# Order of the rough pieces, place of the shift row and PSUM operands on VectorE in a two-layer attention kernel

## The reference

```python
# x: (4, 128, 64, 64); per image N = 4096 positions, C = 128 channels
# layer 0: 64 inner channels
g     = einsum('ic,bcn->bni', g_w, xf) + g_b
theta = einsum('ic,bcn->bni', theta_w, xf) + theta_b
phi   = einsum('ic,bcn->bin', phi_w, xf) + phi_b[:, None]
p     = softmax(einsum('bni,bim->bnm', theta, phi), axis=-1)
y     = einsum('bnm,bmi->bni', p, g).transpose(0, 2, 1)
mid   = einsum('ci,bin->bcn', W_w, y) + W_b[:, None] + xf
# layer 1: 128 channels, x is mid
q, k, v = Wq x + bq,  Wk x + bk,  Wv x + bv
out   = x + softmax(q^T k * 128 ** -0.5) v
```

## Time and profile before

| what | value |
|---|---|
| median of 3 executions | 3499.48 us (3497.35 to 3500.27) |
| the profiled execution | 3494.88 us |
| its span, first to last instruction | 3493.1 us |
| mean granted TensorE clock | 0.991 |
| busy: PE, PEld, DVE, ACT, POOL | 3376.9, 2104.6, 2234.2, 1678.5, 2985.2 us |
| share of the chain that ended last | PE 89%, issue 4%, DVE 3%, POOL 2%, ACT 1% |

### The profile page before, as it was taken

One profiled execution on the slowest core, in us unless ns is written; L12 is line 12 of the kernel. 1 busy time (PEld: TensorE's weight loads), 2 busy tenths in 40 slices (PEclk: granted clock), 3 DMA queues, 4 the chain that ended last, 5 costly groups with the idle time before them and its releaser, 6 DMA issues.

```text
span 3493.1 us, 46688 instructions
## 1 busy us (share of the span) xinstructions
PE 3376.9 (97%) x13124; PEld 2104.6 (60%) x13124; DVE 2234.2 (64%) x3029; ACT 1678.5 (48%) x2241; POOL 2985.2 (85%) x1366
## 2 busy tenths in 40 slices
PE   7999999999999989999999999999999999999998
PEld 4555466666655546666655555666665555566665
DVE  4555577777655557777755555777775555577775
ACT  4454444444444444445444444444444445444444
POOL 4888789898988869899888886989899888698898
PEclk9999999999999999999999999999999999999999
DMA  1000000000000000000000000000000000000000
GB/s 42 13 18 19 28 7 22 15 22 16 19 16 18 13 29 13 19 15 22 13 19 19 18 16 23 16 16 21 16 19 13 19 18 16 19 13 10 18 11 11
DMA packets 34038, 61.73 MB, mean 18 GB/s; under 512 B 5280, under 2 KB 5920, under 8 KB 33568
## 3 DMA queue, kind: packets, MB, share of 16 engines
q1 hardware_dynamic: 33824, 59.23, 5.5%
HBM read 42.44 MB, written 16.78 MB: 17 GB/s over the span
## 4 chain that ended last, share of the span: by engine, by line
PE 89%; issue 4%; DVE 3%; POOL 2%; ACT 1%; SPq 0%; DVEq 0%; DMA 0%; ACTq 0%; POOLq 0%
PE acc_out L472 15%; PE rough L399 15%; PE acc_out L456 13%; PE scores L421 7%; PE scores L424 7%; PE scores L426 6%; PE scores L430 6%; PE scores L427 6%; DVE piece_max L788 2%; PE acc_out L442 2%; PE acc_out L444 2%; PE acc_out L443 2%; POOL sums L281 2%; PE rough L381 2%; PE acc_out L493 1%
## 5 line engine op out<-in xcount | busy, mean ns | idle before, releaser
L281 POOL TENSOR_TENSOR sums<-sums,probs 128x1024 f32<-128x1024 f32 x886 | 2130.6, 2405 | 152.7 <-ACT probs L713 114.3
L788 DVE TENSOR_REDUCE piece_max<-rough 128x1 f32<-128x512 f32 x2024 | 1309.6, 684 | 679.9 <-PE rough L399 665.2
L805 DVE TENSOR_TENSOR probs<-scores,shift_rows 128x1024 f32<-128x1024 f32 x512 | 626.1, 1223 | 494.4 <-PE scores L430 459.9
L713 ACT ACTIVATE probs<-scores 128x1024 f32<-128x1024 f32 x512 | 524.7, 1026 | 707.8 <-PE scores L424 707.8
L706 ACT ACTIVATE probs<-probs 128x1024 f32<-128x1024 f32 x512 | 539.4, 1054 | 516.8 <-DVE probs L805 516.5
L907 POOL TENSOR_TENSOR p_lo<-probs,p_hi 128x1024 fp32r<-128x1024 f32 x192 | 462.7, 2410 | 176.9 <-ACT probs L706 176.6
L472 PE MATMUL acc_out<-probs,v_vals 128*128 128x512 f32 x1280 | 603.0, 593 | 0.0
L456 PE MATMUL acc_out<-probs,g_vals 128*64 128x512 f32 x2048 | 495.0, 605 | 0.0
L426 PE MATMUL scores<-qry_a,k_hi 128*128 128x512 f32 x1024 | 494.6, 483 | 0.0
L421 PE MATMUL scores<-qry_a,phi_a 128*128 128x512 f32 x1024 | 438.7, 428 | 0.0
L705 ACT ACTIVATE p_hi<-probs 128x1024 fp32r<-128x1024 f32 x192 | 203.3, 1059 | 445.7 <-DVE probs L805 360.9
(11 more groups left out here) (97 smaller groups left out, 3113.0 us busy)
## 6 DMA issues: line engine op xcount, KB each, us to landing
x_q<-x SPq DMA_DIRECT2D x32, 256.0 KB, 2.7
x_res<-x SPq DMA_DIRECT2D x32, 256.0 KB, 3.0
mid<-mid_new SPq DMA_DIRECT2D x32, 256.0 KB, 2.2
x_q<-mid SPq DMA_DIRECT2D x32, 256.0 KB, 2.7
x_res<-mid SPq DMA_DIRECT2D x32, 256.0 KB, 3.2
out<-result SPq DMA_DIRECT2D x32, 256.0 KB, 2.3
x_kv<-x SPq DMA_DIRECT2D x24, 256.0 KB, 2.7
probs<-x SPq DMA_DIRECT2D x2, 1024.0 KB, 6.2
```

Source lines behind the costliest of these rows:

```text
L281: eng.tensor_tensor(sums[:, parity], sums[:, parity], probs[:, s % P_BUFS], ALU.add).then_inc(s_plus, 1)
L788: nc.vector.reduce_max(piece_max[:, t, c:c + 1], src, AX.X).then_inc(s_reduced, 1)
L805: nc.vector.tensor_tensor(probs[:, s % P_BUFS].rearrange("p (h c) -> p h c", c=QB), scores[:, s % 2].rearrange("p (h c) -> p h c", c=QB), ...
```

## The change

Three things are altered. In layer 0, at even steps from 2 on, PE makes the step's first two pieces ahead of its scores; odd steps and step 0 are as before. The shift row moves from ahead of the scores of step 15 to behind them, in both layers (so the pair of waits on take_v or take_g and the wait for the diagonal move with it). And four small operands of VectorE are moved to PSUM: query_max to the first four columns of `rough`, the reciprocals to four columns of the block's output bank, and layer 1's normalised output to that bank instead of `result`; the wait for the store of `result` moves to the operation that now first writes it. Because query_max stands in a bank that the next piece overwrites, the first piece of a block that follows a turn (or the start) waits for the diagonal.

```diff
+        query_max = rough[:, 0:SUB]
...
-        query_max = sb("query_max", [P, SUB])
-        rcol = sb("rcol", [P, SUB])
...
                     if m == 0:
 
                         pe.wait_ge(h_q, st.g + 2)
+                        if st.prev is None:
+                            pe.wait_ge(s_diag, st.g + 1)
...
                 for s in range(GROUPS):
-                    if s == ROW_AT and st.nxt is not None and not st.turn:
-                        if st.kv:
-                            pe.wait_ge(h_v, st.nth)
-                        if st.phi_g:
-                            pe.wait_ge(h_g, (st.b + 1) * BLOCKS + st.i + 1)
-                        shift_row(st.g + 1, 1 - st.parity)
...
-                    score_group(st.layer, st.prev, st.g, st.nth, st.nth - 1, st.parity, s)
-                    if st.nxt is not None:
+                    pieces_first = st.layer == 0 and s > 0 and s % BATCH != BATCH_AT
+                    if pieces_first:
                         for _ in range(min(at[s], 2)):
                             piece()
+                    score_group(st.layer, st.prev, st.g, st.nth, st.nth - 1, st.parity, s)
+                    if st.nxt is not None and not pieces_first:
+                        for _ in range(min(at[s], 2)):
+                            piece()
+                    if s == ROW_AT and st.nxt is not None and not st.turn:
+                        if st.kv:
+                            pe.wait_ge(h_v, st.nth)
+                        if st.phi_g:
+                            pe.wait_ge(h_g, (st.b + 1) * BLOCKS + st.i + 1)
+                        shift_row(st.g + 1, 1 - st.parity)
...
             def shift(g, parity):
 
                 dve.wait_ge(s_reduced, (g + 1) * PIECES + 1)
-                nc.vector.reduce_max(query_max[:], piece_max[:], AX.X).then_inc(s_qmax, 1)
+                nc.vector.reduce_max(query_max, piece_max[:], AX.X).then_inc(s_qmax, 1)
                 dve.wait_ge(s_qmax, g + 1)
                 nc.vector.tensor_tensor(
                     diag[:, parity].rearrange("p (t c) -> p t c", c=P),
                     neg_ident[:].unsqueeze(1).to_broadcast([P, SUB, P]),
-                    query_max[:].unsqueeze(2).to_broadcast([P, SUB, P]), ALU.mult).then_inc(s_diag, 1)
+                    query_max.unsqueeze(2).to_broadcast([P, SUB, P]), ALU.mult).then_inc(s_diag, 1)
...
-                nc.vector.reciprocal(rcol[:].unsqueeze(2), den).then_inc(s_rcol, 1)
+                rcol = acc_out[:, parity, 2 * SUB:3 * SUB]
+                nc.vector.reciprocal(rcol.unsqueeze(2), den).then_inc(s_rcol, 1)
                 dve.wait_ge(s_rcol, g + 1)
-                nc.vector.tensor_copy(rparts[:, 0], rcol[:]).then_inc(s_rparts, 1)
+                nc.vector.tensor_copy(rparts[:, 0], rcol).then_inc(s_rparts, 1)
                 dve.wait_ge(s_rparts, 2 * g + 1)
-                nc.vector.tensor_tensor(rparts[:, 1], rcol[:], rd(rparts[:, 0]), ALU.subtract).then_inc(s_rparts, 1)
+                nc.vector.tensor_tensor(rparts[:, 1], rcol, rd(rparts[:, 0]), ALU.subtract).then_inc(s_rparts, 1)
...
-                    dve.wait_ge(s_stored, 16 * nth + 16)
-                    nc.vector.tensor_tensor(result[:], o_sb[:], acc_out[:, parity], ALU.mult).then_inc(s_norm, 1)
+                    nc.vector.tensor_tensor(acc_out[:, parity], o_sb[:], acc_out[:, parity],
+                                            ALU.mult).then_inc(s_norm, 1)
...
                     dve.wait_ge(s_norm, g + 1)
-                    src, dst, bias = result[:], result[:], V_B
+                    dve.wait_ge(s_stored, 16 * nth + 16)
+                    src, dst, bias = acc_out[:, parity], result[:], V_B
```

## The result

The changed kernel takes 3435.44 us (median of 4 executions, 3433.24 to 3435.71), the kernel before 3498.53 beside it; the ratio is 0.9818, 95% interval 0.9801 to 0.9835: 63 us less, against 66 forecast. The two profiled executions, 3494.88 and 3435.51, are 59.4 apart.

The account below looks back on a forecast made before the run. PE, busy 97%, bounds the kernel, so only time PE loses counts. Savings of 57.1 (24 middle blocks), 3.8, 1.9, 1.4 and 2 sum to 66.2 us: 3499.5 - 66.2 = 3433.3, rounded 3433; 8-in-10 range 3418 to 3460.

Parts of the forecast that it names:

- part 1: Layer 0, pieces first at even steps: PE's waits at steps 3, 5, 7, 13 go, 1.08 us a block gained.
- part 2: Layer 0, step 8: three pieces in a row for two banks, the third waits; net loss 0.5 us a block.
- part 3: Row behind step 15's scores: layer 0's wait for the diagonal goes whole, 1.8 us a block; layer 1 nothing.
- blocks 0 of layer 0: First blocks of images 2 to 4 save 1.3 us each, 3.8 in all; the very first block 1.9.
- turn blocks: Four blocks whose end POOL's last addition sets: 0.35 us gained each, 1.4 in all.
- The diagonal's length: VectorE's diagonal ahead of the row: 0.69 us with an operand in PSUM, where it took up to 2.86.
- Part 4: Reciprocals and layer 1's output in PSUM: 2 us saved in the last image, between 0 and 5.
- Part 5: New wait for the diagonal at the first piece after a turn: nothing, at most 0.5 us, four times.
- The waits of the pieces: Rival: the pieces' waits only move, part 1 gives nothing and part 2 costs 0.5; 3463 us, 9%.
- The long diagonal: Rival: the PSUM operand doesn't free the diagonal, the row waits 0.73 us in 27 blocks; 3453 us, 8%.
- POOL did not become the bound: Rival: POOL becomes layer 0's bound, its lag reaching PE at every denominator, half the gain lost; 3468 us, 5%.
- ACT's later copies: Rival: ACT's queue behind the later row delays each layer 0 block's first piece; 14 us slower, 3514 us, 3%.

Follow-up runs that it names:

- the run with the row early: The changed kernel with the shift row put back ahead of the scores of step 15: 3434.49 us, ratio 0.9820.
- step 8 put back: The changed kernel with step 8's pieces put back behind its scores: 3424.30 us, ratio 0.9795.
- thirds at even steps: The changed kernel with layer 0's third pieces at steps 6, 8, 10, 12 in place of 7, 8, 11, 13: 3403.41 us, ratio 0.9734.
- one piece at step 0: The changed kernel with layer 0's third pieces at even steps, one piece at step 0 and three at step 4: 3394.93 us, ratio 0.9714.
- the run with the last image written out: The changed kernel with the loop over blocks 1 to 4 written out in the last image's layer 1 alone: 3427.15 us, ratio 0.9804.

## Why the prediction was right, point by point
**The sum.** The term of the 24 middle blocks, 2.38 us each, measured 2.37. Its parts can be read from the runs: the operands alone save 1.67 a block (40.0 over 24); the order of the pieces on top of them, as in the run with the row early, 0.65 more, where part 1 less part 2 had 0.58; the late row 0.06 more. So the wait of 1.8 us went, but part 3 of the prediction credited the row with it, and the operands had earned nearly all of it.

That 3433 was met to 2 us is in part luck. The sum came out 6.8 us too large: 66.2 for 59.4. The forecast then took it off the median of 3499.48, 4.6 us above the profiled execution, and in later groups of 7 to 9 executions the kernel before had 3495.7 to 3496.6, no more than 2 us above it. Of what is missing, 4.0 us are in the blocks 0 of layer 0, 4.2 are the clock's in three places (below) and 0.4 in the middle and turn blocks; 1.7 go the other way, in layer 1, where the blocks save that much more than the prediction gave them.

**Part 1 and 2** stand: the pairs of steps 3, 7 and 13 take 0.55 us to the values, the run of three costs 0.83 (1.62 us measured for 1.63), and step 8 put back regains 0.45 for the 0.47 expected. Where part 2 failed is "step 12 doesn't have this: keys or the values' projection stand behind step 11's third piece in most blocks". Block 0 of an image has no values to project, and so has a second run of three. PE's timeline after, step 11 to 12 of such a block:
```profile
931.44 0.73 PE L398 MATMUL rough<-phi_a,qry_a 128*128 128x512 f32 x2
932.73 0.50 PE L398 MATMUL rough<-phi_a,qry_a 128*128 128x512 f32 x1 [0.55 <-DVE piece_max L793]
933.07 0.40 PE L420 MATMUL scores<-qry_a,phi_a 128*128 128x512 f32 x1
```
It costs 0.83 us four times, 3.3 of the 4.0 us by which blocks 0 fell short. The very first block, for which the prediction gives 1.9 without a working, has no values at step 1 either: there four pieces stand in a row, and PE waits another 0.56 us.

**The diagonal's length** came out as taken, 0.69 us. The Trainium skill ("SBUF — State Buffer", Who interferes with whom) has it that an operation of VectorE with at most one input in SBUF, outside the modes that use both ports, doesn't contend with GpSimd. By that rule, the trace agrees: 691 ns at most in 64 executions, against 2791 with the one operand back in SBUF. The prediction left the condition out, and the cast of four columns shows it: one input, in SBUF, and still it took 0.38 to 2.12 us in 33 of its 64 executions before; from PSUM it takes 0.16 in all. What the prediction did not see is that the stretch depends on where in POOL's operation the diagonal begins, and that the new order alone moves it to a harmless place. It therefore treated as separate what is one wait with three remedies: alone they save 47, 25 and 48 us, together 63.

**Part 4.** 2 us were forecast for the last image and 0.91 came, though its mechanism stands. The wait of 1.33 us behind the stretched cast and subtraction is in the fourth block, which took 62.29 us. In the run with the operands alone that wait is gone, the block takes 60.09, and blocks 1 to 6 together 2.67 us less. In the changed kernel the wait is gone too, but the block takes 61.94, since the clock fell in it. The first lines are the changed kernel's, the last two the same place in the kernel before:
```profile
3136.48 1.10 PE L398 MATMUL rough<-k_hi,qry_a 128*128 128x512 f32 x2 [1.46 <-DVE piece_max L793]
3137.41 3.20 PE L471 MATMUL acc_out<-probs,v_vals 128*128 128x512 f32 x4
3139.62 1.42 PE L425 MATMUL scores<-qry_a,k_hi 128*128 128x512 f32 x1
...
3197.24 1.88 PE L472 MATMUL acc_out<-probs,v_vals 128*128 128x512 f32 x4
3198.55 0.80 PE L426 MATMUL scores<-qry_a,k_hi 128*128 128x512 f32 x1
```
Behind the stall of the loop's return the changed kernel's PE works at 1.2 GHz for 3.41 us; four value matmuls take 2.21 us to the next start in place of 1.31, and 1.8 us are lost in all. The stall itself costs 1.8 us before and 2.0 after; no term of the prediction had it, and it is why the block stays 2 us above its neighbours' 58.1 even where the clock holds.

**Part 5** and the turn blocks (1.24 for 1.4) held.

**What was left out.** The TensorE clock, in three places, of which the fourth block of the last image is one (1.8 us). Granted clock in windows of the kernel before (the end, and behind a turn), after the window first its length, then busy time of PE, PEld, DVE, ACT, POOL, then the clock, the DMA share and GB/s:
```profile
1288.00:1298.00 10.00, 6.91 (x18) 4.25 (x18) 4.65 (x8) 1.87 (x4) 1.27 (x1) 0.51 0.35 109
...
3479.00:3484.00 5.00, 4.27 (x13) 1.94 (x12) 3.14 (x3) 0.60 (x1) 1.26 (x1) 1.00 0.00 0
```
and of the changed kernel:
```profile
1253.70:1267.30 13.60, 8.04 (x19) 5.18 (x20) 5.00 (x10) 4.83 (x12) 1.28 (x1) 0.50 0.26 82
...
3137.90:3140.60 2.70, 2.70 (x5) 1.15 (x4) 1.45 (x3) 2.00 (x2) 0.24 (x1) 0.50 0.00 0
...
3417.70:3421.10 3.40, 3.40 (x8) 1.98 (x7) 1.65 (x2) 0.00 (x0) 1.54 (x1) 0.50 0.00 0
```
Around the second turn PE works at 1.2 GHz (0.50) for 13.6 us where it had 10 us of it, and in the last block for 3.4 us where it had none. Matmuls in that stretch start 0.43 us apart in place of 0.23, and 1.34 us are lost there. Layer 1's first blocks lose 1.05 us over the four images, gaining where the slow stretch behind the turn is shorter (the first image) and losing where it is longer. PE's idle times ahead of the stretch in the last block are nearly the same in both kernels (2.43 and 2.44 us). In the fourth block of the last image an idle time of 1.45 us was followed by the fall in the run with the row alone, one of 1.69 us with thirds at even steps, and none followed 1.42 us with the pieces alone or 1.69 us with one piece at step 0. So why the clock falls in one kernel and not in the other is open, and wasn't tried. In the run with the last image written out the 1.33 us of the last block came back.

**The rivals.** None came true. The waits of the pieces didn't just move, as the pairs' 0.55 us show. The long diagonal would have given 3453; even with both inputs in SBUF the new order avoids it. POOL did not become the bound, not at 42.85 us a block either. ACT's later copies delayed nothing.

## What to carry to other kernels
A stall in a kernel that repeats exactly may be a matter of phase between two engines that share something: look at what the other engine is doing when the stretched operation begins and when that ends, and expect parts of a change to be worth less together than alone. Space the users of a double-buffered bank evenly, and count runs of three in every variant of the block, the first and last ones too, for these have less in between. Before a difference of 1 to 2 us is put down to an edit, look at the granted clock in the stretch where it arises.

## What the runs showed of the hardware that was not expected
- In the kernel before the diagonal, both inputs in SBUF, took 0.69 us where POOL was idle at its start and 0.78 to 2.86 us when it began during an operation of POOL: it ended 0.55 us behind the end of that one, in each of 59 executions. Of the four-column casts and subtractions 61 were stretched and ended 0.02 to 0.03 us behind POOL's. An addition of POOL that began during a stretched diagonal took 2.7 us in place of 2.4, and 2.8 in the run with the pieces alone.
- The return of a two-turn loop left DVE idle for 4.68 us between two instructions, in the last image, and for 4.3 to 4.9 us at that place in every kernel here that has the loop there. PE lost 2.0 us by it in the changed kernel, and 1.8 more by the clock behind it. The same loop in the other images shows nothing of this in its blocks.
- Four columns cast from PSUM took 0.16 us, from SBUF 0.17 where not stretched: a small operand in PSUM cost VectorE nothing.
- The clock of TensorE fell to 1.2 GHz for 3.4 us in the last block of one kernel and not of the other, which cost 1.34 us, and for 3.4 us behind 1.46 us of idle time in the last image's fourth block, which cost 1.8.
